# A GNN and LSTM block on one core: constant multiplies in TensorE's waits, degree sums on VectorE, and another order on GpSimd

## The reference

```
h = relu(layernorm(x))
h = relu(adj @ (h @ Wg0 + bg0));  h = relu(adj @ (h @ Wg1 + bg1))
for p in 1..4:  cut the tokens into windows of p, run an LSTM(p) over each window,
                put its last state in place of the window's last token
x = x + h
h = relu(layernorm(x))
An = adj + I
deg = sum(An, axis=0) + sum(An, axis=1) - diagonal(An)
Ahat = An * rsqrt(deg)[:, None] * rsqrt(deg)[None, :]
z = relu(batchnorm((Ahat @ h) @ W1.T + b1))        # 256 wide, statistics over all tokens
x = x + batchnorm(z @ W2.T + b2)
```

## Time and profile before

| | |
|---|---|
| median of 3 runs | 567.07 us (564.61 to 568.53) |
| the profiled execution | 565.18 us |
| its span, first to last instruction | 563.4 us |
| mean granted TensorE clock | 0.973 of full |
| busy: TensorE, VectorE, ScalarE, GpSimd | 504.7, 413.8, 353.2, 197.3 us |

### The profile page before, as it was taken

How to read it: one execution, slowest core, us unless ns; L and a number is a source line. 1 busy time by engine, 2 the same in 40 slices (tenths; PEclk the granted TensorE clock), 3 DMA queues, 4 the chain that set the end, 5 groups by cost and what they waited for, 6 DMA issues and landing times.

```text
span 563.4 us, 7993 instructions
## 1 busy us (share of the span) xinstructions
PE 504.7 (90%) x2697; PEld 430.3 (76%) x2697; DVE 413.8 (73%) x957; ACT 353.2 (63%) x679; POOL 197.3 (35%) x299
## 2 busy tenths in 40 slices
PE   3998998797898999999989999999779998895866
PEld 3787787797897789988977889889557998673546
DVE  3646667788857888678578887775786888877867
ACT  3544765555567667566676575675766677456863
POOL 4502021304400647055005471440052514247940
PEclk9998999798999999999999999999999999997997
DMA  7300030000001011102011101010910000600007
GB/s 224 114 19 2 0 94 19 2 19 1 19 20 58 37 38 56 58 1 75 31 65 56 37 38 57 2 56 1 366 64 19 20 2 19 224 1 0 1 1 298
DMA packets 17837, 31.21 MB, mean 55 GB/s; under 512 B 1498, under 2 KB 6020, under 8 KB 17796
## 3 DMA queue, kind: packets, MB, share of 16 engines
q1 hardware_dynamic: 16804, 30.17, 15.7%
q10 hardware_dynamic: 992, 0.52, 0.4%
HBM read 19.16 MB, written 11.53 MB: 54 GB/s over the span
## 4 chain that ended last, share of the span: by engine, by line
PE 49%; issue 21%; DVE 12%; POOL 9%; ACT 5%; POOLq 3%; DMA 1%; DVEq 0%; ACTq 0%
PE gate_ps L1093 10%; PE gate_ps L1095 9%; PE gate_ps L1094 9%; PE pre_ps L1094 3%; PE pre_ps L1095 3%; PE pre_ps L1093 3%; POOL x_pre L371 3%; PE post_ps L1093 3%; POOL z_back L426 3%; PE post_ps L1095 2%; PE post_ps L1094 2%; POOLq L369 2%; ACT gate L651 2%; DVE cell L935 1%; PE pre_ps L1154 1%
## 5 line engine op out<-in xcount | busy, mean ns | idle before, releaser
L641 ACT ACTIVATE gate<-gate_ps,gate_bias 128x256 f32<-128x256 f32 (+2 forms) x312 | 164.0, 562 | 45.4 <-PE gate_ps L1095 43.8
L1093 PE MATMUL gate_ps<-by_class_hi,wih_hi 128*128 128x256 f32 (+2 forms) x264 | 86.5, 328 | 15.3 <-POOL by_class_lo L390 9.2
L651 ACT ACTIVATE gate<-cell 128x512 f32<-128x512 f32 (+2 forms) x88 | 45.3, 515 | 68.5 <-DVE cell L930 34.8
L1095 PE MATMUL gate_ps<-by_class_lo,wih_hi 128*128 128x256 f32 (+2 forms) x264 | 84.5, 320 | 0.0
L1094 PE MATMUL gate_ps<-by_class_hi,wih_lo 128*128 128x256 f32 (+2 forms) x264 | 84.4, 320 | 0.0
L1093 PEld LDWEIGHTS gate_ps<-by_class_hi,wih_hi 128*128 128x128 f32 x264 | 50.7, 192 | 22.9 <-POOL by_class_lo L390 10.7
L1093 PE MATMUL gate_ps<-hstep_hi,whh_hi 128*128 128x256 f32 (+2 forms) x192 | 60.7, 316 | 0.0
L1095 PE MATMUL gate_ps<-hstep_lo,whh_hi 128*128 128x256 f32 (+2 forms) x192 | 60.5, 315 | 0.0
L1094 PE MATMUL gate_ps<-hstep_hi,whh_lo 128*128 128x256 f32 (+2 forms) x192 | 60.5, 315 | 0.0
L390 POOL TENSOR_TENSOR by_class_lo<-h,by_class_hi 128x256 fp32r<-128x256 f32 (+1 forms) x40 | 36.8, 927 | 55.4 <-ACT by_class_hi L649 55.3
L1094 PEld LDWEIGHTS gate_ps<-by_class_hi,wih_lo 128*128 128x128 f32 x264 | 50.8, 192 | 3.5
(11 more groups left out here) (295 smaller groups left out, 1304.3 us busy)
## 6 DMA issues: line engine op xcount, KB each, us to landing
x_pre<-in_x SPq DMA_DIRECT2D x16, 256.0 KB, 2.7
x<-in_x SPq DMA_DIRECT2D x16, 256.0 KB, 2.7
z_spill<-z_ring SPq DMA_DIRECT2D x8, 512.0 KB, 2.7
z_back<-z_spill SPq DMA_DIRECT2D x8, 512.0 KB, 6.7
x_spill<-x SPq DMA_DIRECT2D x12, 256.0 KB, 2.0
x_back<-x_spill SPq DMA_DIRECT2D x1, 3072.0 KB, 11.2
out<-x_back SPq DMA_DIRECT2D x12, 256.0 KB, 2.3
x<-in_adj SPq DMA_DIRECT2D x1, 1024.0 KB, 6.4
```

The lines of the kernel that those rows point to most:

```text
L641: nc.scalar.activation(gate[:, tile_of(g), gt, 0:size], gate_ps[k % GATE_BANKS][:, 0:size], ACT.Tanh if gt == G_GATE else ACT.Sigmoid, bia ...
L651: nc.scalar.activation(gate[:, tile_of(g), G_GATE, 0:size], cell[:, tile_of(g), 0:size], ACT.Tanh)\
L1093: nc.tensor.matmul(ps, w[0], m[0], start=start, stop=False)
L1095: return nc.tensor.matmul(ps, w[0], m[1], start=False, stop=stop)
```

## The change

It has four parts.

1. `busy(count)`: TensorE multiplies `ones_r` by `bg1_row` into `post_ps`, which nobody reads, `count` times: 11 times at the start before the transposes of `adj`, 20 times before the products that need `bn1`, 16 times before the transposes that need `bn2`.
2. The degrees: `adj` is loaded with four neighbouring rows in each partition, and VectorE adds them up in the prologue with four reductions over 2048 elements (`deg_part`: rows of `adj`, high parts and low parts of its transpose, diagonal). GpSimd combines the four (four small instructions) and takes the power. TensorE's matmuls of L1201 to L1205 and VectorE's L831, L836, L885 and L889 go, except that the four diagonal multiplications of L831 stay in another place. `DINV_DIAG` moves from slot 5 to slot 2, `DINV_ROWS` from slot 7 to slot 4, and `HAT_CHUNK` from slots 8, 11, 14, 17 to 5, 9, 12, 17. The loads of `x1` wait for the reductions instead of for TensorE's sums.
3. GpSimd: a layer norm that stood at slot s now stands after the low part of slot s+1, where slot s+1 has one (`NORMS_AFTER`).
4. The prologue: `stats` of batch 1 stands after the split of `adj`'s first piece and of batch 0's norm.

```diff
+BUSY_FOR_ADJ, BUSY_FOR_BN1, BUSY_FOR_BN2 = 11, 20, 16
-DEG_SUM, DEG_TOKENS, DEG_POW, DINV_DIAG, DINV_ROWS = 3, 3, 4, 5, 7
-HAT_CHUNK = (8, 11, 14, 17)
+DINV_DIAG, DINV_ROWS = 2, 4
+HAT_CHUNK = (5, 9, 12, 17)
+DEG_ROWS, DEG_HI, DEG_LO, DEG_DIAG = range(4)
+def makes_parts(slot):
+    return slot < N_SLOTS and TURNS[slot][2] >= 3 and TURNS[slot][3] + 1 < TURNS[slot][2]
+NORMS_AFTER = [[at for at in (slot - 1, slot) if at >= 0 and makes_parts(at + 1) == (at < slot)] for slot in range(N_SLOTS)]
...
-        PROLOGUE = ([("stats", 0), ("stats", 1), ("bank", 0), ("norm", 0), ("bank", 1), ("bank", 2), ("bank", 3),
+        PROLOGUE = ([("stats", 0), ("bank", 0), ("norm", 0), ("stats", 1), ("bank", 1), ("bank", 2), ("bank", 3),
...
-                     ("bank", 7), (LIN1, 0), (LIN1, 1), (LIN0, 2), ("bank", 8), (AGG0, 3), (AGG1, 0), ("bank", 9),
-                     (LIN0, 3), (LIN1, 2), (AGG1, 1), ("bank", 10)]
+                     ("bank", 7), (LIN1, 0), (LIN1, 1), (LIN0, 2), ("bank", 8), ("deg", DEG_ROWS), (AGG0, 3), ("deg", DEG_HI), (AGG1, 0), ("bank", 9),
+                     (LIN0, 3), (LIN1, 2), ("deg", DEG_LO), (AGG1, 1), ("bank", 10)]
...
-                    + [(LIN1, 3), ("bank", 11), (AGG1, 2), ("bank", 12)]
+                    + [(LIN1, 3), ("bank", 11), ("deg", DEG_DIAG), (AGG1, 2), ("bank", 12)]
...
+            pool.wait_ge(deg_ready, 4)
+            nc.gpsimd.tensor_tensor(deg[:, DEG_ROWS, :], deg[:, DEG_ROWS, :], deg[:, DEG_HI, :], ALU.add)
+            nc.gpsimd.tensor_tensor(deg[:, DEG_LO, :], deg[:, DEG_LO, :], deg[:, DEG_DIAG, :], ALU.subtract).then_inc(deg_sum, 1)
...
+            nc.gpsimd.tensor_tensor(dinv[:, :], deg[:, DEG_ROWS, :], minus_half[:, :], ALU.pow).then_inc(dinv_ready, 1)
...
+                for at in NORMS_AFTER[slot]:
+                    for kind, n in PRE_AFTER[at]:
...
-            sp.dma_start(adj_raw[:, :, :], adj.rearrange("(c p) s -> p c s", p=P)).then_inc(adj_in, 16)
+            sp.dma_start(adj_raw[:, :, :], adj.rearrange("(p c) s -> p c s", c=CHUNKS)).then_inc(adj_in, 16)
...
-                    sp.wait_ge(deg_mm, 1)
+                    sp.wait_ge(deg_ready, 4)
...
+            def deg_part(i):
+                if i == DEG_DIAG:
+                    dve.wait_ge(consts_ready, 3)
+                    for c in range(CHUNKS):
+                        last = nc.vector.tensor_tensor(deg_fix[:, c, :], adj_raw[:, c, c::CHUNKS], ident[:, :], ALU.mult)
...
+                nc.vector.reduce_sum(deg[:, i, :], src, AX.X).then_inc(deg_ready, 1)
...
+            def busy(count):
+                for _ in range(count):
+                    nc.tensor.matmul(post_ps[:, :], ones_r[:, :], bg1_row[:, :], start=True, stop=True)
...
-                        last = nc.tensor.transpose(ps[:, c * P:(c + 1) * P], adj_raw[:, c, i::CHUNKS], ident[:, :])
+                        last = nc.tensor.transpose(ps[:, c::CHUNKS], adj_raw[:, c, i::CHUNKS], ident[:, :])
...
+            pe.wait_ge(consts_ready, 3)
+            busy(BUSY_FOR_ADJ)
...
-                if n == DEG_SUM:
-                    pe.wait_ge(fix_ready, 1)
...
-                    for c in range(CHUNKS):
-                        nc.tensor.matmul(post_ps[:, :], ones_f[:, :], adj_raw[:, c, :], start=c == 0, stop=False)
-                        for part in adj_t:
-                            nc.tensor.matmul(post_ps[:, :], ones_r[:, :], part[:, c, :], start=False, stop=False)
...
+            busy(BUSY_FOR_BN1)
             pe.wait_ge(z_ready, 2 * BATCHES)
...
+            busy(BUSY_FOR_BN2)
             pe.wait_ge(z2_ready, BATCHES)
```

More of the change, by code:

```diff
@@ L179, in build @@
         dinv = sb("dinv", [P, CHUNKS])
-        deg = sb("deg", [P, CHUNKS])
+        deg = sb("deg", [P, 4, CHUNKS])
         hat = pair("hat", [P, CHUNKS, T])
@@ L395, in _ @@
                     later_class(r, chain, p, step + 1)
[L396 to L405, removed]
+                for at in NORMS_AFTER[slot]:
+                    for kind, n in PRE_AFTER[at]:
+                        if kind == "stats":
+                            norm_pre(n)
+                    for kind, n in POST_AFTER[at]:
+                        if kind == "stats":
+                            norm_post(n, y_post)
             for n in range(LATE, LATE + 2):
@@ L609, in _ @@
                     normed(i, x_pre[:, i % 2, :], nrm[i % 2], pre_y, pre_nhi)
-                elif kind != "stats":
+                elif kind not in ("stats", "deg"):
                     pre_unit(kind, pre_number(i, kind), i, prologue_ps(i), i % 2)
@@ L821, in pre_unit @@
                 low(dst[1], src, dst[0], relu=func == ACT.Relu).then_inc(pre_lo, 1)
+            def deg_part(i):
[3 more added lines that the diff above has]
+                        last = nc.vector.tensor_tensor(deg_fix[:, c, :], adj_raw[:, c, c::CHUNKS], ident[:, :], ALU.mult)
+                    last.then_inc(diag_part, 1)
+                    dve.wait_ge(diag_part, 1)
+                if i == DEG_HI:
+                    dve.wait_ge(setup_hi, CHUNKS)
+                if i == DEG_LO:
+                    dve.wait_ge(setup_lo, CHUNKS)
+                src = {DEG_ROWS: adj_raw, DEG_HI: adj_t[0], DEG_LO: adj_t[1], DEG_DIAG: deg_fix}[i][:, :, :]
+                if i in (DEG_HI, DEG_LO):
+                    src = f32(src)
+                nc.vector.reduce_sum(deg[:, i, :], src, AX.X).then_inc(deg_ready, 1)
             for kind, i in PROLOGUE:
@@ L825, in _ @@
                     bank_lo(i)
-                    if i == len(BANKS) - 1:
-                        dve.wait_ge(adj_in, 16)
-                        dve.wait_ge(consts_ready, 3)
-                        for c in range(CHUNKS):
[L831 to L838, removed]
+                elif kind == "deg":
+                    deg_part(i)
                 elif kind == "rows":
@@ L880, in hat_steps @@
             def hat_steps(n):
[L881 to L885, removed]
-                                                       ident[:, :], ALU.mult)
-                    last.then_inc(deg_part, 1)
-                    dve.wait_ge(deg_part, 1)
-                    nc.vector.reduce_sum(deg[:, :], hat_t[:, :].rearrange("p (c q) -> p c q", c=CHUNKS), AX.X)\
-                        .then_inc(deg_ready, 1)
                 if n == DINV_DIAG:
@@ L1164, in _ @@
                     bank(i)
-                elif kind not in ("stats", "norm", "rows"):
+                elif kind not in ("stats", "norm", "rows", "deg"):
                     if kind == LIN0 and i == 0:
@@ L1195, in deg_steps @@
             def deg_steps(n):
-                if n == DEG_SUM:
-                    pe.wait_ge(fix_ready, 1)
-                    pe.wait_ge(pre_lo, 3 * EARLY)
-                    for c in range(CHUNKS):
-                        nc.tensor.matmul(post_ps[:, :], ones_f[:, :], adj_raw[:, c, :], start=c == 0, stop=False)
-                        for part in adj_t:
-                            nc.tensor.matmul(post_ps[:, :], ones_r[:, :], part[:, c, :], start=False, stop=False)
-                    for c in range(CHUNKS):
-                        last = nc.tensor.matmul(post_ps[:, c * P:(c + 1) * P], ones_f[:, :], deg_fix[:, c, :],
-                                                start=False, stop=c == CHUNKS - 1)
-                    last.then_inc(deg_mm, 1)
                 if n == DINV_ROWS:
                     pe.wait_ge(dscale_ready, 1)
+                    pe.wait_ge(pre_lo, 3 * EARLY)
                     for c in range(CHUNKS):
```

8 lines of the change are left out of this document (6 added, 2 removed).

## The result

| | before | changed |
|---|---|---|
| median of 6 runs | 567.13 us (564.61 to 568.53) | 558.51 us (558.21 to 559.76) |
| ratio | | 0.9855, 95% interval 0.9833 to 0.9878 |
| profiled execution, its span | 565.18, 563.4 us | 558.27, 556.1 us |
| mean granted clock there | 0.973 | 0.993 |
| gain forecast, gain measured | | 11.0 us, 8.6 us (6.9 between the two profiled executions) |

The first line is from the changed kernel's page and answers to the earlier trace rows: TensorE is busy for as long as before, since the constant multiplications fill what the degree sums and the stretches at half clock left, and VectorE has 5 us more.

A forecast was written before the change was run, and what follows sets the result against it. TensorE, busy 504.7 of 563.4 us, was taken as the bound. Gains of 4.6 + 3.7 + 1.4 + 1.3 = 11.0 us off the 567.07 median gave 556.1 us, range 551 to 562.

The forecast's parts named there:

- the degree sums with slot 10: Round 0: without TensorE's sums and GpSimd's wait, slot 10 starts at 97.6 instead of 102.17; gain 4.6 us.
- slot 16 of round 0: TensorE's 2.38 us wait for GpSimd's low part goes whole, with the half clock after it; gain 3.7 us.
- round 3: Slot 16 of round 3: TensorE's 1.91 us wait for GpSimd goes; gain 1.4 us (0 to 1.9).
- the end: Constant multiplications before `bn2` keep full clock, additions come faster until stores bound; gain 1.3 us (0.7 to 1.8).
- The prologue: Start: three reductions fit idle time; the fourth, with four multiplications, delays the first gates 0.6 us (0.5 to 1.5).
- Slots 10 to 14: Round 0: moved pieces of `Ahat` stand beside full TensorE slots, with no gap as before; cost 0.
- the clock at slot 10: Round 0: half clock after the wait lost 2.1 us before; nothing counted, 0 and 2.1 kept as ends.
- the third rival: The constants don't hold the clock, as `bg1_row` is mostly zeros; the end gains nothing: 557.4 us, chance 0.10.
- Before `bn1`: GpSimd paces the stage from 511.8 to 538.7, so a faster TensorE gives 0.
- the eleven at the start: Before the transposes of `adj`: transposes come earlier, but batch 1's `stats` is the next link; gain 0.
- half of it is given back: Rival: clock falls at two of four new waits, another wait replaces slot 16's; gain 5.3, 561.8 us, chance 0.20.

The follow-up runs named there:

- a4: Changed kernel with the old order of GpSimd's norms and of the first `stats`, and no constant multiplications: 561.33 us, 0.9930.
- a3: Kernel before the change with GpSimd's new order of norms alone: 568.20 us, 1.0033.
- c4: Changed kernel, new GpSimd order in round 0 alone, constant multiplications at five more TensorE waits (holds), pieces of `Ahat` in slots 5, 12, 17, 20: 551.51 us, 0.9734.
- c3: Changed kernel, new GpSimd order in round 0 alone, five holds (constant multiplications): slots 0, 10 of round 0, 6, 16 of round 3, behind last slot: 553.19 us.
- c1: The changed kernel run once more, nothing altered: 558.71 us, 0.9858.
- c2: Changed kernel with the pieces of `Ahat` in slots 5, 12, 17 and 20 instead of 5, 9, 12 and 17: 559.05 us, 0.9867.
- b3: Changed kernel with the pieces of `Ahat` back in slots 8, 11, 14 and 17: 558.26 us, 0.9855.
- b1: Changed kernel with GpSimd's new order in round 0 alone and the old order in rounds 1 to 3: 559.36 us, 0.9863.
- b4: Kernel before the change with GpSimd's new order, and the pieces of `Ahat` in slots 8, 10, 12 and 17: 566.82 us, 0.9996.
- a1: Changed kernel with all three counts of constant multiplications at zero: 558.83 us, 0.9881.

## Why the prediction was right, and where its steps were wrong

The forecast was 556.1 us in a range of 551 to 562; measured were 558.5. The direction was right, and so was the mechanism of the two largest terms, the degree sums with slot 10 (4.6) and slot 16 of round 0 (3.7). By the medians 8.6 of 11.0 us came, in the account 7.3. There round 3 missed by 2.5 us, the end by 1.3, the clock at slot 6 of round 3 by 1.3, and 1.3 more went in small steps. The prologue and the clock at the first gates gave back 0.9 and 1.6, which nobody had forecast: that the total came as near as it did is in part luck. Step by step:

**The prologue: wrong.** It was charged 0.6 us and lost nothing. Three reductions took what was forecast, the fourth did not, for it runs over the four 128-wide diagonals alone: 512 elements, not 2048 as the description of the change and the prediction say.

```profile
39.44 2.28 DVE L856 TENSOR_REDUCE deg<-adj_t_lo 128x4 f32<-128x2048 f32 x1
45.23 1.26 DVE L846 TENSOR_TENSOR y_post<-x,ident 128x128 f32<-128x128 f32 x4
46.53 0.69 DVE L856 TENSOR_REDUCE deg<-y_post 128x4 f32<-128x512 f32 x1
```

The first gates started between 50.1 and 51.6 us in the profiled executions with the degrees on VectorE, and at 51.5, 51.1 and 53.0 in those without, so any cost is smaller than that scatter.

**The degree sums and the wait at slot 10: right.** From slot 1 to slot 10 the lead grew by 4.9 us, against 5.2. As forecast, the next bounds are VectorE's waits at slots 6 (1.19), 8 (1.29) and 10 (2.00), and the sums' 6.08 us are kept in part. a4 shows that without the order GpSimd's wait of 4.94 remains, a3 that without the degrees the order still moves slot 10 by 2.9.

**Slots 10 to 14: the size right, the reason wrong.** The prediction said that the moved pieces of `Ahat` stand "beside full slots of TensorE", and took nothing for them. The step came out at -0.35 us, but TensorE's slots were not full: behind slot 10 it waited three times (0.89 at 104.81, 0.63 at 110.53 and 0.74 us at 121.90), where before it had no wait until 128.4. VectorE's timeline in the changed kernel:

```profile
98.46 0.51 DVE L774 TENSOR_TENSOR hstep_lo<-gate,hstep_hi 128x340 fp32r<-128x340 f32 x1
98.89 0.69 DVE L891 TENSOR_TENSOR z_ring<-adj_t_hi,adj_t_lo 128x512 f32<-128x512 f32 x1
...
101.59 0.69 DVE L774 TENSOR_TENSOR hat_lo<-z_ring,hat_hi 128x512 fp32r<-128x512 f32 x1
102.20 0.51 DVE L939 TENSOR_TENSOR cell<-gate,cell 128x340 f32<-128x340 f32 x1
...
105.22 0.51 DVE L774 TENSOR_TENSOR hstep_lo<-gate,hstep_hi 128x340 fp32r<-128x340 f32 x1
```

In c4, with no piece there, the same cell follows the same `hstep_lo` at once, and the first two of the three waits are gone:

```profile
97.95 0.51 DVE L774 TENSOR_TENSOR hstep_lo<-gate,hstep_hi 128x340 fp32r<-128x340 f32 x1
98.38 0.51 DVE L939 TENSOR_TENSOR cell<-gate,cell 128x340 f32<-128x340 f32 x1
...
101.57 0.51 DVE L774 TENSOR_TENSOR hstep_lo<-gate,hstep_hi 128x340 fp32r<-128x340 f32 x1
```

From slot 9's `hstep_lo` to slot 10's it is 6.8 us with the piece and 3.6 without. c3 and c4 differ in nothing else, and their leads say the same: at slot 9 6.8 and 7.7, at slot 14 6.2 and 9.1, so 2.0 us more for c4; the medians differ by 1.7. Once TensorE's waits are gone VectorE paces these slots. This is also why the clock at slot 10, for which the prediction kept 0 to 2.1, was worth 0.4. It fell there in c1 (its slot 10 and the window over it), and not in the changed kernel's profile:

```profile
94.90 0.52 PE L1107 MATMUL gate_ps<-by_class_hi,wih_hi 128*128 128x340 f32 x1 [2.00 <-issue]
```

```profile
94.00:99.00 5.00, 4.10 (x16) 4.13 (x17) 4.34 (x8) 2.99 (x7) 3.63 (x6) 0.66 0.00 0
```

Both led by 6.5 us at slot 14, from 4.4 at slot 8 in c1 and 4.0 in the other. The half rate and the piece run beside each other. Taking away one of them gives nothing that lasts (c2, whose clock fell); taking both gives the 2 us (c4).

**Slot 16 of round 0: right** (3.8 against 3.7), but for a reason that the prediction did not give: a3 and b3 show that the order alone leaves 2.15 us for `hstep_lo`, and that it goes only since the piece of slot 14 has moved. Between these two sets of slots the pieces' place does not matter, as b3 says: what they cost at 9 they cost at 14. Away from both it does (c4).

**Round 3: wrong, in place and in sign.** The wait of the earlier trace rows at 469.15 stands at slot 18, not 16: slot 16's own `hstep_lo` was made at 466.07 already, slot 18's at 474.59. It did go, and yet 1.1 us were lost instead of 1.4 won. The changed kernel's TensorE, VectorE and GpSimd there:

```profile
458.52 0.28 PE L1107 MATMUL gate_ps<-by_class_hi,wih_hi 128*128 128x256 f32 x1
467.00 0.36 PE L1107 MATMUL gate_ps<-by_class_hi,wih_hi 128*128 128x256 f32 x1 [1.52 <-issue]
```

```profile
461.84 0.42 DVE L774 TENSOR_TENSOR hstep_lo<-gate,hstep_hi 128x256 fp32r<-128x256 f32 x1
463.71 0.96 DVE L941 TENSOR_TENSOR gate<-gate 128x256 f32<-128x256 f32 x1
466.47 0.42 DVE L774 TENSOR_TENSOR hstep_lo<-gate,hstep_hi 128x256 fp32r<-128x256 f32 x1
```

```profile
463.61 0.78 POOL L410 TENSOR_TENSOR by_class_lo<-h,by_class_hi 128x256 fp32r<-128x256 f32 x1 [2.41 <-ACT by_class_hi L667]
```

Slot 18 starts 10.6 us earlier than before, but its `hstep_lo` only 8.1: VectorE has its instructions for slots 17 and 18 in a row and was the later one already. The slots behind it then wait for `hstep_lo` (1.52 us at slot 20). And VectorE's own pace drops where it begins while GpSimd's low part runs: the multiplication at 463.71 took 0.96 us, and 0.42 alone. The Trainium skill (GPSIMD Engine Reference, Specifications) says that GpSimd's way to SBUF is shared with VectorE, with contention for instructions with two inputs there; the row agrees. In these rows it is the instruction that begins second that takes longer. Some eight microseconds earlier the same multiplication began 0.05 us ahead of a low part, and there GpSimd's instruction was the long one:

```profile
455.30 0.41 DVE L941 TENSOR_TENSOR gate<-gate 128x256 f32<-128x256 f32 x1
455.35 0.95 POOL L410 TENSOR_TENSOR by_class_lo<-h,by_class_hi 128x256 fp32r<-128x256 f32 x1 [2.62 <-ACT by_class_hi L667]
```

From slot 4 to slot 19 of round 3, VectorE's instructions that began while a low part ran took 3.3 us (changed kernel) and 3.2 us (c1) longer in all than the shortest of their shape, and 1.8 us with the old order (before, b1, c3). With the old order in rounds 1 to 3 and the clock held, the lead went from 10.0 us (slot 15, round 0) over 10.9 (round 3) to 10.9 at the last step (c3); with the new order, in c1, from 10.4 over 10.6 to 8.0, 1.7 of it by the clock. So from there the new order costs some 1.6 us, of which about 1.0 lie in round 3. That comes from two traces; the time alone (b1) did not show it.

**The end: the size.** 1.3 were forecast; between the two profiled executions it is 0.0, without a slow issue it is 1.0. The constants do hold the clock, although `bg1_row` is mostly zeros: the third rival falls (the clock read 1.00 over the last transposes in all eight executions with them, and 0.50 over part of them in the other six). Before `bn1` they saved nothing that shows, as forecast; and the eleven at the start nothing either.

**The clock.** The prediction took it as given by the kernel. It is not: after the same wait of 2.00 us before slot 10 it fell in c1 and not in the changed kernel, and at the first gates it fell in the kernel before and in b1, b3 and b4, but not in the changed kernel, a1 to a4, c1 or c2. The 1.6 us won there are luck of this pair of executions. The Trainium skill (TensorE: Matmul & The Clock Gate, What's actually happening) says that the gate's intervals run free of the kernel's start; these rows fit that, and no run here tests it. In rows, a fall cost 1.3 to 2.0 us where TensorE set the pace (first gates, slot 6 and slot 18 of round 3, behind the last slot) and 0.4 or less where VectorE or GpSimd did (slot 10, `bn1`). c3 differs from b1 in the five holds alone, and its trace has none of these falls: 0.9863 to 0.9763, 1.0% or 5.7 us with intervals clear of each other, two thirds of what the whole change gave. Of the rivals, "half of it is given back" was right about the clock and the new waits, and wrong about the amount.

Open: why one store issue of some executions takes over 1 us, and which executions lose the clock at a wait that others pass. No kernel with stores further apart, or on a second queue, was run.
